# Relation stage of a four-layer graph network: the leaky rows made by ScalarE and GpSimd instead of VectorE

## The reference

```python
proj = jnp.einsum('ni,rio->nro', nfeat, relation_weight)
t_r, h_r = proj[src, etype], proj[dst, etype]
att = jnp.sum(t_r * jnp.tanh(h_r + efeat), axis=-1)
a = softmax of att over the edges with one dst
h_nb = jax.ops.segment_sum(nfeat[src] * a[:, None], dst, num_segments=n)
out = leaky_relu((nfeat + h_nb) @ res_fc_w.T, 0.01) + leaky_relu(nfeat * h_nb @ res_fc2_w.T, 0.01)
```

## Time and profile before

| | us |
|---|---|
| median of 3 runs | 5080.18 |
| the profiled execution, as timed | 5083.74 |
| its span in the trace | 5081.9 |
| relation stage in the trace | about 2711 to 4045 |

### The profile page before, as it was taken

One profiled execution on the slowest core, in us unless ns is written; L12 is line 12 of the kernel. 1 busy time (PEld: TensorE's weight loads), 2 busy tenths in 40 slices (PEclk: granted clock), 3 DMA queues, 4 the chain that ended last, 5 costly groups with the idle time before them and its releaser, 6 DMA issues. The chain is left out here.

```text
span 5081.9 us, 79008 instructions
## 1 busy us (share of the span) xinstructions
PE 4321.3 (85%) x24557; PEld 2936.6 (58%) x24557; DVE 3370.7 (66%) x6947; ACT 1894.7 (37%) x3531; POOL 2834.3 (56%) x2859
## 2 busy tenths in 40 slices
PE   5989998999989997588887889899898677777666
PEld 1268887788867776166675455555555444444444
DVE  9967777667768887567765788888887633333332
ACT  0056666444445444011211245455454322222222
POOL 0066664776756665776613544444442167777777
PEclk9989999999989999666656989899899689988998
DMA  1079997899866675444423434344342132222221
GB/s 38 1 237 287 288 287 237 217 231 237 230 176 186 189 192 147 92 114 112 116 62 84 98 89 101 92 96 94 93 96 68 47 67 66 65 64 55 65 66 29
DMA packets 1124517, 649.04 MB, mean 128 GB/s; under 512 B 907542, under 2 KB 940589, under 8 KB 1124104
## 3 DMA queue, kind: packets, MB, share of 16 engines
q1 hardware_dynamic: 1036296, 555.84, 39.9%
q0 software_dynamic: 87808, 88.16, 8.8%
HBM read 384.69 MB, written 261.63 MB: 127 GB/s over the span
## 5 line engine op out<-in xcount | busy, mean ns | idle before, releaser
L2215 POOL DMA_INDIRECT r_got<-x_table,slot_idx x392 | 435.6, 1111 | 743.9 <-DVE r_both_t L2439 312.5
L1084 POOL DMA_INDIRECT o_rows<-in_x_dram,dst_idx x392 | 370.2, 944 | 468.6 <-POOLq L347 265.8
L2530 POOL DMA_INDIRECT m_rows<-x_table,slot_idx x392 | 376.1, 960 | 235.9 <-issue 118.8
L2669 DVE TENSOR_TENSOR_SCAN m_both<-m_keep,m_both,m_rows_t 128x512 f32<-128x512 bf16 x97 | 124.2, 1280 | 564.9 <-PE m_rows_t L2592 564.9
L1994 POOL DMA_INDIRECT t_got<-x_table,slot_idx x392 | 384.5, 981 | 188.7 <-issue 109.4
L1535 POOL DMA_INDIRECT b_rows<-h_table,slot_idx x392 | 369.6, 943 | 207.6 <-issue 91.5
L1346 POOL DMA_INDIRECT a_got<-node_table,src_idx x392 | 375.5, 958 | 194.8 <-DVE a_conv L1482 56.9
L2538 POOL DMA_INDIRECT out_dram<-s_res,put_out x392 | 390.6, 996 | 137.3 <-issue 111.7
L2314 PE MATMUL r_source_t<-r_masked,rel_pair 64*128 64x512 f32 x980 | 467.1, 622 | 0.0
L2316 PE MATMUL r_own_t<-r_masked,rel_pair 64*128 64x512 f32 x980 | 467.0, 622 | 0.0
L1238 ACT ACTIVATE s_square<-s_sum_t 128x256 f32<-128x256 f32 x392 | 149.4, 381 | 786.6 <-PE s_sum_t L2068 385.5
(11 more groups left out here) (402 smaller groups left out, 12370.7 us busy)
## 6 DMA issues: line engine op xcount, KB each, us to landing
x_table<-n_res SPq DMA_DIRECT2D x196, 256.0 KB
n_rows<-x_table SPq DMA_DIRECT2D x196, 256.0 KB
x_table<-s_res SPq DMA_DIRECT2D x294, 128.0 KB
node_table<-n_wide SPq DMA_DIRECT2D x98, 272.0 KB, 4.0
h_table<-n_conv SPq DMA_DIRECT2D x98, 256.0 KB
x_table<-s_res SPq DMA_DIRECT2D x98, 256.0 KB
r_feats<-in_edge_attr_dram SPq DMA_DIRECT2D x390, 64.0 KB
n_rows<-in_x_dram SPq DMA_DIRECT2D x97, 256.0 KB
```

What stands on the lines that cost most here:

```text
L1084: nc.gpsimd.indirect_dma_start(out=rows[:, n % 4, t, :], out_offset=None, in_=x, in_offset=bass.IndirectOffsetOnAxis(ap=dst_idx[:, n * TIL ...
L2215: nc.gpsimd.indirect_dma_start(out=got[:, n % RING, t, :], out_offset=None, in_=x2_table, in_offset=bass.IndirectOffsetOnAxis(ap=slot_idx[ ...
L2530: nc.gpsimd.indirect_dma_start(out=rows[:, n % 4, t, 0:D], out_offset=None, in_=x3_table, in_offset=bass.IndirectOffsetOnAxis(ap=slot_idx[ ...
```

## The change

`plain` becomes two tiles. ScalarE's `take` makes two results from `r_out_t`, a copy scaled by 0.01 and a ReLU scaled by 0.99, and each raises `plain_made` by one. `leak` is no longer a step of VectorE; it is a step of GpSimd, an add of the two tiles, called between `gather` and `pair_up` with lag X + 6. GpSimd's list runs two turns ahead of TensorE's in block numbers, so `leak` of block m stands in front of `pair_up` of block m + 15 and after the four gathers of block m + 21.

```diff
-            plain = sb(c, "r_plain", [P, EDGE_BLOCK])
+            plain = sb(c, "r_plain", [P, 2, EDGE_BLOCK])
-            plain_made, leaked = sig.get("rising"), sig.get("leaked")
+            plain_made, leaked = sig.get("rising", 2), sig.get("leaked")
@@ GpSimd
-                    over_turns((gather, 0, BLOCKS), (pair_up, 6, BLOCKS))
+                    def leak(m):
+                        pool.wait_ge(plain_made[m], plain_made.done(m))
+                        if m >= 2:
+                            pool.wait_ge(norm.summed[m - 2], norm.summed.done(m - 2))
+                        nc.gpsimd.tensor_tensor(leaky[:, m % 2, :], plain[:, 0, :], plain[:, 1, :], ALU.add).then_inc(leaked[m], 1)
+                    over_turns((gather, 0, BLOCKS), (leak, X + 6, BLOCKS), (pair_up, 6, BLOCKS))
@@ ScalarE, take(m)
-                        nc.scalar.activation(plain[:, :], out_t[:, :], ACT.Copy).then_inc(plain_made[m], 1)
+                        nc.scalar.activation(plain[:, 0, :], out_t[:, :], ACT.Copy, scale=SLOPE).then_inc(plain_made[m], 1)
+                        nc.scalar.activation(plain[:, 1, :], out_t[:, :], ACT.Relu, scale=1.0 - SLOPE).then_inc(plain_made[m], 1)
@@ VectorE
-                    def leak(m):
-                        dve.wait_ge(plain_made[m], plain_made.done(m))
-                        if m >= 2:
-                            dve.wait_ge(norm.summed[m - 2], norm.summed.done(m - 2))
-                        nc.vector.scalar_tensor_tensor(out=leaky[:, m % 2, :], in0=plain[:, :], scalar=SLOPE, in1=plain[:, :],
-                                                       op0=ALU.mult, op1=ALU.max).then_inc(leaked[m], 1)
-                               (powers, X + 4, BLOCKS), (leak, X + 3, BLOCKS),
+                               (powers, X + 4, BLOCKS),
```

## The result

The changed kernel takes 5124.24 us (median of 3 runs, 5119.12 to 5124.95) against 5080.18: slower, with a ratio of 1.0083 (95% interval 1.0060 to 1.0106), 44 us. The profiled execution took 5119.12 us, with a span of 5117.2. One of the four executions of the kernel with useless matmuls 5, 8 and 10 (see the experiments) took 14,236 us at a mean granted clock of 0.28 and is left out of the medians and intervals; nothing here explains it.

The account below looks back on a forecast made before the run. TensorE bounds plain turns, VectorE's late scan delays two of seven, one small chain binds the last part. +5.5 us over 11 periods and +4.0 in the last part make +9.5: 5093.2 profiled, 5090 beside the runs; range 5071 to 5116.

Parts of the forecast that it names:

- the clock case with a full period's delay: Longer 1.2 GHz stretches of TensorE with a full period's delay; left out of the range, with a table load, at 0.08.
- the third gather at 0.94: GpSimd, plain turns: without VectorE's `leak` beside it the gather takes 0.94 us instead of 1.48, freeing GpSimd 0.54 earlier.
- no table load: ScalarE's added ReLU needs no table load of 1.28 us; bound otherwise 13 turns by 1.3 us, 17 us.
- the last part: Final 115 us, bound by one small chain: second activation +0.5, removal -0.14, +0.36 us a turn, +4.0 in sum.
- The late scan: VectorE in a slow turn: line 1839 held over both GpSimd instructions; +0.7 to +1.1 us, taken as +0.9.
- a pair that holds `mix`: One turn before the late scan: GpSimd late by about 1 us, its pair holding VectorE's `mix` for 0.45 us.
- the next two turns: After the late scan: removed `leak` gives 0.15, half the delay is won back; 0.5 of 0.95 us per period.
- The rival on the clock: TensorE's 1.2 GHz stretch lasts half as long again, 6.9 us plus 3.4, half lost; 19 us, 5109; chance 0.13.
- the plain turn: `match` starts 0.5 us late, 0.37 hidden as slack; two of three plain turns pay 0.1 each, +0.2 per period.
- The rival on `match`: Third gather keeps 1.48 us or add takes 1.5: plain turns +0.6 per period, all 0.9 arrives; +21, 5101; chance 0.18.
- Other side: VectorE's two-input steps before the late scan run ahead of GpSimd: -1.9 us in each of 11 periods, 5063; chance 0.12.

Follow-up runs that it names:

- useless matmuls 5, 8 and 10: Kernel before, plus 5, 8 and 10 unused 256-column matmuls between `match` and `join` in three turns of seven: 5035.64 us, ratio 0.9912.
- half the change: Against the kernel before: ScalarE's two results, added by VectorE, 5085.32 us; one ScalarE activation, GpSimd adding that tile to itself, 5104.46 us.
- filled kernels: Useless matmuls where TensorE idles, three turns of seven: kernel before (5, 4, 10) 5024.47 us, (5, 8, 10) 5035.64; changed kernel (6, 8, 11) 5079.63.
- pair first: Changed kernel with GpSimd's `pair_up` ahead of `leak`: 5116.04 us, ratio 1.0057; with useless matmuls (6, 8 and 11) too, 5058.54 us.
- clock held: Useless matmuls in three turns of seven keep TensorE's clock at 1.00: changed kernel (6, 8, 11) 5079.63 us, kernel before (5, 8, 10) 5035.64.
- best filling: Kernel before with 5, 4 and 10 useless matmuls in three turns of seven: 5024.47 us, ratio 0.9891.
- short-add kernels: Changed kernel, GpSimd adding only 8 of 512 columns: in one block of seven 5110.70 us, in two 5097.66, in every block from 7 on 5078.13.
- short add in one block of seven: Changed kernel, GpSimd adding only 8 of 512 columns in block 1 modulo 7: 5110.70 us, ratio 1.0052.

## Why the prediction was wrong

Predicted were 5090 us and a range to 5116; the median is 5124. The direction was given 0.49 and came true; no rival had this size. The range had left out the clock case with a full period's delay, at a chance of at most 0.08, and that is the nearest to what happened.

**Right.** The add at 1.28 us, the third gather at 0.94 (3281.90 and others), leak and pair back to back, line 1839 held for both, no table load, and the last part: 6.00 us a turn was worked out as 6.03, and +5.2 us in all stands against +4.0. The late scan was sized +0.7 to +1.1 and cost +0.62: the first figure of that step, 1.28 - 0.6 = 0.68, was the close one, and what was added for a pair that holds `mix` doesn't show, for turn 2 keeps its 10.46. The experiments with half the change confirm which half did what: ScalarE's costs the last part, GpSimd's the periods and some 6 us ahead of them.

The prediction found the trace in agreement with the rule that the second of the two engines to issue is blocked. The size agrees. The order doesn't: line 1839 began 0.14 us ahead of the pair by its record and was the one held.

**The step that failed: "the next two turns".** It said that a later start leaves TensorE less work at half speed and that "half of the delay is won back", so that 0.2 + 0.9 - 0.15 = 0.95 us counts 0.5 per period. Nothing was won back. The join of turn 4 came after 2.91 us of idle TensorE instead of 2.39, and the low-clock stretch behind it lasted 9.6 us instead of 7.0. That of turn 6 began later in the turn and reached one source matmul more. Turns 4 and 6 lost 1.38 + 0.24 = 1.62 us, where the step had -0.45. The rival on the clock said that a stretch would last half as long again (6.9 us and 3.4 more; it was 6.8 and 3.4 more) and cost 1.7 per period, close to 1.62. It had a chance of 0.13, and its waits were the forecast's, which were themselves too small. That the clock carries this loss is shown by the filled kernels: with it at 1.00, turn 6 is 10.98 us in either kernel, and turn 4 loses only 0.68. Why the stretch of turn 4 grew stays open. The longer idle time doesn't settle it: with the pair first, 3.02 us idle were followed by either length, and in the tenth period of the changed kernel itself 2.89 us idle by the short one (a turn of 13.68).

**The second fault in the same step: a hold not seen.** It gave VectorE -0.15 us in turn 5 for the removed `leak`. In its place line 1914 was held by the new add: +0.90 on the instruction, +0.75 on the turn. The add isn't even needed for it: with no leaky step at all the pair holds line 1914 for the same 1.31 us, and the turn takes 16.39. What brings it about is the removal. It makes two gathers shorter, so that GpSimd is free 1.3 us earlier in this turn (9.47 us into it instead of 10.80). The prediction had the shorter gather, and followed it through the plain turn alone. I had also taken only instructions with two SBUF inputs to be open to such a hold; line 1914 reads one. The Trainium skill ("SBUF — State Buffer", Who interferes with whom) lists `tensor_scalar` among the operations that can take the ports shared with GpSimd. This trace agrees, 1.31 us against 0.41.

**Undersized: the plain turn.** One turn of seven pays 0.45 us, not two 0.1 each. The step expected `match` 0.5 us late, with 0.37 of that hidden in a slack in front of the scan's copy. There was no such slack: the join starts 1.33 us after `match` before and after the change, so the 0.45 us by which `match` starts later reach the join in full. Pair first takes this away. The rival on `match` had 0.6 per period from this place, and gave as its reason a longer gather or add, neither of which came.

**Sum.** Waits 0.45 + 0.62 + 0.75 = 1.82 per period against 0.95, and clock +1.62 against -0.45: 3.44 against 0.5. (The split at turn 4 is of the unfilled kernels; with the clock held 0.68 of its 1.38 are there as a wait.) Ten such periods make 34.4 us; the eleventh, in which the gathers end, took 1.4 less than before (80.70 against 82.07), so 33.1, and 3.5 ahead of them. With the last part's 5.2 and 0.1 behind it that makes the 42 us of the stage.

**With the clock held**, the loss doesn't vanish: the usual period still loses 2.25 us, and against the best filling (83.82, with the pair first 85.86) 2.04 even without the wait of `match`: 0.62 in turn 3, 0.68 in turn 4 and 0.75 in turn 5. As one loss goes, line 1868 held in turn 4, hidden behind the slow matmuls before, comes out.

**Other side.** The rival in which VectorE gets ahead was priced at 1.9 us. The short-add kernels show that it exists: line 1839 ran in 0.68 us and turn 3 in 12.46. What decides is that GpSimd's work then meets a later softmax step (line 1909 or 1914), a consequence that the rival left out.

Not tried: GpSimd's add in the 1.45 us in which it waits for the masks. It would need a block's leaky rows a turn later, and so a shift of all steps behind them.

## What to carry to other kernels

Moving an elementwise step from VectorE to an idle GpSimd is paid for by the VectorE instructions that run beside it, so list those that the moved step will meet, with its full length and those queued back to back behind it, and don't take one-input steps as safe. Removing a step moves the other engine too: where it slowed a gather, GpSimd now comes earlier, and meets other instructions. Where rows show TensorE's clock low behind an idle time, give none of a delay back, and allow for a longer low stretch (here 10.2 us instead of 6.8). The total of such a kernel can hide single waits, so hold the clock high before pricing them. Here the cheap gain lay elsewhere: useless matmuls just as long as the idle time in three of seven turns brought 56 us against the kernel before, more than the 19 that removing the step altogether brought.

## What the runs showed of the hardware that was not expected

- A VectorE scan that by its record was already 0.53 us under way was held until two GpSimd instructions queued back to back had ended: 4.10 us instead of 1.27 (short add in one block of seven). Between the two, VectorE never got its turn.
- `tensor_scalar` on 7 x 512 f32 went from 0.41 to 1.31 us beside GpSimd's add, and GpSimd's two instructions then took 1.47 and 1.44 instead of 1.27; the reciprocal of the same size stayed at 3.34 in every turn of every kernel.
- GpSimd's issue of an indirect gather took 0.94 us, and 1.48 where VectorE's two-input `leak` started beside it, and 1.73 where it was issued during VectorE's scan of line 1909; with `leak` gone from VectorE the third and fourth gathers took 0.94 in the periods, but for a handful.
- After the same 3.02 us of idle TensorE, turn 4 had a mean clock of 0.75 in five periods and 0.66 in four (pair first, clock not held).
- GpSimd's add of a tile to itself took 1.06 us, of two tiles 1.29, and on 8 of the 512 columns 0.28 on average.
